# Two graph layers on one core: the second layer sums neighbours first and weights the sums per row tile

## What is computed

```
# layer 0 (T = 350 largest of each row are kept; no row of these inputs has more)
sim     = tanh(adj * adj)
new_adj = sim where adj > 0, at most T largest of a row
h2      = tanh(x @ W_proj + b_proj)
x1      = layernorm(x + relu(new_adj @ (h2 @ W_gcn) + b_gcn))
# layer 1
pos  = (adj > 0) @ x1
neg  = (adj < 0) @ x1
node = concat(pos, neg) @ node_weight + node_bias * diag(adj)
edge = (adj @ x1) @ edge_weight + edge_bias * diag(adj)
out  = layernorm(x1 + node + edge)
```

## Time and profile before

| | |
|---|---|
| runs | 654.3, 657.14, 657.41 us; median 657.14 |
| profiled execution | 656.15 us, span 653.9 us |
| TensorE, products / weight loads | 615.0 us (94%) / 348.3 us |
| VectorE | 492.2 us (75%) |
| ScalarE | 449.1 us (69%) |
| GpSimd | 122.3 us (19%), all in layer 0 |
| DMA | 130.62 MB, 200 GB/s over the span |
| mean granted TensorE clock | 0.981 |
| layer 0 products | 37.3 to 284.2 us |
| layer 1 | 284.2 us to the end |

### The profile page before, as it was taken

How to read it: one execution, slowest core, us unless ns; L and a number is a source line. 1 busy time by engine, 2 the same in 40 slices (tenths; PEclk the granted TensorE clock), 3 DMA queues, 4 the chain that set the end, 5 groups by cost and what they waited for, 6 DMA issues and landing times.

```text
span 653.9 us, 6778 instructions
## 1 busy us (share of the span) xinstructions
PE 615.0 (94%) x2016; PEld 348.3 (53%) x2016; DVE 492.2 (75%) x689; ACT 449.1 (69%) x302; POOL 122.3 (19%) x71
## 2 busy tenths in 40 slices
PE   6599599999999999999999999999999999999994
PEld 3454244444444444476655555555555555556993
DVE  2462797979797797995758978779688687786845
ACT  2295769797878879641688878787675858676740
POOL 0242446454454535400000000000000000000000
PEclk9699799999999999999999999999999999999997
DMA  9999999999999994000099888788675867765000
GB/s 210 335 209 245 243 331 321 267 305 258 295 257 311 259 286 130 1 1 0 25 254 238 256 248 232 240 220 249 189 212 161 240 198 203 203 181 145 1 17 18
DMA packets 140313, 130.62 MB, mean 200 GB/s; under 512 B 8579, under 2 KB 140294, under 8 KB 140294
## 3 DMA queue, kind: packets, MB, share of 16 engines
q1 hardware_dynamic: 72118, 65.23, 38.1%
q10 hardware_dynamic: 68176, 65.15, 36.0%
HBM read 128.27 MB, written 2.10 MB: 199 GB/s over the span
## 4 chain that ended last, share of the span: by engine, by line
PE 61%; issue 16%; POOL 13%; DVE 5%; ACT 2%; ACTq 2%; DMA 1%; POOLq 0%; SPq 0%; DVEq 0%
PE acc L950 29%; POOL a_cols L305 13%; PE acc L952 8%; PE acc L951 8%; DVE a_cols L495 3%; PE acc L892 3%; PE stage L914 2%; PE stage L970 2%; PE acc L970 2%; ACTq L380 2%; PE stage L843 1%; PE stage L836 1%; DMA early<-in_x_dram 1%; ACT a_cols L424 1%; DVE root L550 1%
## 5 line engine op out<-in xcount | busy, mean ns | idle before, releaser
L495 DVE STREAM_TRANSPOSE a_cols<-a_rows 128x2048 f32<-128x2048 f32 x128 | 293.1, 2302 | 88.8 <-PE acc L952 43.3
L892 PE MATMUL acc<-a_cols,rhs 128*128 128x512 f32 x512 | 224.9, 597 | 7.3 <-ACT a_cols L424 7.3
L950 PE MATMUL acc<-a_cols,rhs 128*128 128x512 f32 x448 | 229.0, 592 | 0.0
L951 PE MATMUL acc<-masks,pos_hi 128*128 128x512 f32 x224 | 178.5, 797 | 0.0
L448 ACT ACTIVATE a_rows<-a_rows 128x4096 f32<-128x4096 f32 x32 | 116.0, 3624 | 74.8 <-DVE a_cols L495 58.4
L892 PEld LDWEIGHTS acc<-a_cols,rhs 128*128 128x128 f32 x512 | 96.7, 192 | 123.9 <-issue 115.7
L305 POOL TENSOR_TENSOR a_cols<-a_cols 128x1024 f32<-128x1024 f32 x64 | 121.5, 1898 | 154.4 <-DVE a_cols L495 154.4
L424 ACT ACTIVATE a_cols<-a_cols 128x2048 f32<-128x2048 f32 x64 | 122.3, 1911 | 17.4 <-POOL a_cols L305 15.8
L451 ACT ACTIVATE a_rows<-a_rows 128x4096 f32<-128x4096 f32 x32 | 116.0, 3624 | 2.9
L950 PEld LDWEIGHTS acc<-a_cols,rhs 128*128 128x128 f32 x448 | 83.9, 189 | 19.3
L420 ACT ACTIVATE a_cols<-a_cols 128x1024 f32<-128x1024 f32 x64 | 67.1, 1049 | 35.4 <-DVE a_cols L495 18.5
(11 more groups left out here) (83 smaller groups left out, 326.4 us busy)
## 6 DMA issues: line engine op xcount, KB each, us to landing
a_rows<-in_adj_dram SPq DMA_DIRECT2D x120, 512.0 KB, 8.2
a_rows<-in_adj_dram ACTq DMA_DIRECT2D x120, 512.0 KB, 8.5
early<-in_x_dram SPq DMA_DIRECT2D x8, 256.0 KB, 6.3
out_dram<-n_rows ACTq DMA_DIRECT2D x7, 256.0 KB, 8.5
out_dram<-n_rows ACTq DMA_DIRECT2D x2, 128.0 KB, 1.8
w_pne<-n_L_gnn_node_weight_dram SPq DMA_DIRECT2D x1, 128.0 KB
w_pg<-in_L_gnn_W_proj_dram ACTq DMA_DIRECT2D x1, 64.0 KB, 2.7
w_pg<-in_L_gnn_W_gcn_dram ACTq DMA_DIRECT2D x1, 64.0 KB, 3.3
```

The source lines that it names most:

```text
L495: nc.vector.transpose(half_out(hs), half_in(s, h % HALVES)).then_inc(turned[layer], 1)
L892: last = nc.tensor.matmul(acc[parity][:], rhs[:, b, :], a_cols[:, h % HSLOTS, k, :], start=(b == 0), stop=(b == BLOCKS - 1))
L950: nc.tensor.matmul(acc[parity][:], rhs[:, b, :], cols, start=(b == 0), stop=False)
L951: nc.tensor.matmul(acc[parity][:], pos_hi[:, b, :], mask, start=False, stop=False)
```

## The change

The second layer is computed in another order: (A x1) W_edge + ((A > 0) x1) W_node, where it was A (x1 W_edge) + (A > 0)(x1 W_node). So `operands` is gone, x1 itself is the stationary operand, and each chunk's two sums (now in two banks, `acc` and `acc_m`) are copied to SBUF and multiplied with the weights tile by tile (`weigh`). A chunk is no longer 512 neighbouring rows but, for each of 16 sets, 32 rows out of 256, so that its rows are, in the order in which the columns lie on partitions, four whole blocks (c, c + 8, c + 16, c + 24). x lies in `x_rows` in that order, with rows on partitions; the layer norm writes x1 there, and nothing is transposed back. ScalarE rounds it into `x1_hi`, VectorE forms `x1_lo`, once per chunk in layer 0.

Also: GpSimd squares 1280 of 2048 elements of a half, where it was 1024, and ScalarE 768; x comes in 16 DMAs of 128 KB, half on SP and half on ScalarE's queue; ScalarE issues chunk 0's first piece before its first activation; the head goes through six banks in another order; the diagonal comes in four DMAs; the stores go out on SP, in four DMAs each.

```
-    SQ_POOL = HB // 2
+    SQ_POOL = HB * CH * 5 // 8
...
+        adj_sets = adj.rearrange("(r c i) k -> (c i) r k", c=CHUNKS, i=SQ)
+        x_blocks = x.rearrange("(q b j) f -> q j b f", q=QUARTERS, j=SQ)
+        def quarter_in(c, s, q):
+            return adj_sets[bass.ds(c * SQ, SQ), :, q * QUARTER + s * PCOLS:q * QUARTER + (s + 1) * PCOLS]
...
# ScalarE
+            def relu_out(chunk):
+                c, q, parity = chunk
+                act.wait_ge(half_used[0], HPC * (c + 1))
+                nc.scalar.activation(by_tile(z_t[:]), by_set(acc[parity][:]), ACT.Relu, bias=b_col[:, 1:2])\
+                    .then_inc(z_ready, 1)
+            def high_part(chunk):
+                c = chunk[0]
+                act.wait_ge(normed, c + 1)
+                nc.scalar.copy(rows_at(x1_hi, c), rows_at(x_rows, c)).then_inc(hi_ready, 1)
...
+                    nc.scalar.activation(rest, rest, ACT.Square).then_inc(squared_act, 1)
+                    if h == HPC - 1 and before:
+                        high_part(before)
...
-                if before:
-                    x1_back(before)
...
+                    if s == 1 and before:
+                        keep_sums(before)
+                    if s == 0 and not before:
+                        high_part(LAST)
# VectorE
+            def residual0(chunk):
+                c = chunk[0]
+                dve.wait_ge(rows_ready, c + 1)
+                nc.vector.tensor_tensor(y_rows[:], to_rows[:], rows_at(x_rows, c), ALU.add).then_inc(y_ready, 1)
+                dve.wait_ge(y_ready, c + 1)
+            def low_part(chunk):
+                c = chunk[0]
+                dve.wait_ge(hi_ready, c + 1)
+                nc.vector.tensor_tensor(rows_at(x1_lo, c), rows_at(x_rows, c), rows_at(x1_hi, c).bitcast(f32),
+                                        ALU.subtract).then_inc(lo_ready, 1)
...
                     turn(0, chunk[0], h)
-                    if h == 3 and before:
+                    if h == 4 and before:
                         residual0(before)
-                    if h >= 5 and before:
-                        norm0(before, h - 5)
+                        norm0(before, 0)
+                    if h == 5 and before:
+                        norm0(before, 1)
+                    if h == 6 and before:
+                        norm0(before, 2)
+                    if h == 7 and before:
+                        low_part(before)
...
+                nc.vector.tensor_copy(by_tile(sm_t[:]), by_set(acc_m[parity][:])).then_inc(sums_m_kept, 1)
# TensorE
                     last.then_inc(half_used[0], 1)
-                    if h == 1 and before:
-                        turn_to_rows(0, before[0])
-                    if h == 5 and before:
-                        turn_x1_back(before)
+                    if h == 0 and before:
+                        turn_to_rows(before)
...
+            def products(sums, sums_m, b, cols, mask):
+                nc.tensor.matmul(sums, x_rows[:, b, :], cols, start=(b == 0), stop=(b == BLOCKS - 1))
+                nc.tensor.matmul(sums_m, x1_hi[:, b, :], mask, start=(b == 0), stop=False)
+                return nc.tensor.matmul(sums_m, x1_lo[:, b, :], mask, start=False, stop=(b == BLOCKS - 1))
+            def weigh(rows, at, tiles):
+                for k in range(tiles):
+                    nc.tensor.matmul(rows[:, k, :], blk(z_t, at + k), w_pne[:, 2, :], start=True, stop=False)
+                    last = nc.tensor.matmul(rows[:, k, :], blk(sm_t, at + k), w_pne[:, 0, :], start=False, stop=True)
+                last.then_inc(rows_ready, 1)
+            def chunk_rows(chunk):
+                c = chunk[0]
+                pe.wait_ge(sums_kept, c + 1)
+                pe.wait_ge(sums_m_kept, c + 1)
+                pe.wait_ge(y_ready, CHUNKS + c)
+                weigh(to_rows, 0, TILES)
...
+                    if h == 0:
+                        chunk_rows(before)
```

More of the change, by code:

```diff
@@ L396, in _ @@
-            before_layer0(0)
-            def x1_back(chunk):
-                c, q, parity = chunk
-                act.wait_ge(cols_ready, c + 1)
-                nc.scalar.copy(nodes(feat_t[:], q, parity), sets(to_cols)).then_inc(x1_ready, 1)
+            act.wait_ge(proj_loaded, 32)
+            for n, (kind, g) in enumerate(USES):
+                if by_dve[n]:
+                    continue
+                act.wait_ge(staged, n + 1)
+                if kind == "hid":
+                    nc.scalar.activation(group(h_t, g), bank_of(n), ACT.Tanh, bias=b_col[:, 0:1])\
+                        .then_inc(stage_act, 1)
+                    if g in (1, 3, 6):
+                        load_piece(0, 1 + (1, 3, 6).index(g))
+                else:
+                    nc.scalar.copy(rhs[:, g * TILES:(g + 1) * TILES, :],
+                                   bank_of(n).rearrange("p (b f) -> p b f", f=F)).then_inc(stage_act, 1)
@@ L672, in layer1 @@
                         before_layer1(h)
+                    if h == 3 and before:
+                        keep_sums_m(before)
                     n, hs = turn(1, chunk[0], h)
@@ L676, in layer1 @@
                         .then_inc(masked, 1)
-                    if h == 3 and before:
-                        residual1(before)
                     if h >= 5 and before:
@@ L856, in turn_to_rows @@
+            def turn_to_rows(chunk):
+                c = chunk[0]
+                pe.wait_ge(z_ready, c + 1)
+                if not is_first(c):
+                    pe.wait_ge(y_ready, c)
                 for k in range(TILES):
@@ L858, in turn_to_rows @@
                 last.then_inc(rows_ready, 1)
-            def turn_x1_back(chunk):
-                c, q, parity = chunk
-                pe.wait_ge(normed, c + 1)
-                if not isinstance(c, int) or c > 0:
-                    pe.wait_ge(x1_ready, c)
-                for k in range(TILES):
-                    last = nc.tensor.transpose(to_cols[:, k * P:(k + 1) * P], n_rows[:, parity, k, :], ident[:])
-                last.then_inc(cols_ready, 1)
             def layer0(chunk, before):
@@ new lines, in chunk_rows, with first_chunk @@
+            def chunk_rows(chunk):
+                c = chunk[0]
+                pe.wait_ge(sums_kept, c + 1)
+                pe.wait_ge(sums_m_kept, c + 1)
+                pe.wait_ge(y_ready, CHUNKS + c)
+                weigh(to_rows, 0, TILES)
+            def first_chunk():
+                parity, late = 0, CHUNKS - 1
+                pe.wait_ge(lo_ready, late)
+                pe.wait_ge(masked, 1)
+                block_products(parity, 0, 0)
+                turn_to_rows(LAST)
+                for k in range(1, HB):
+                    last = block_products(parity, 0, k)
+                last.then_inc(half_used[1], 1)
+                pe.wait_ge(masked, 2)
+                for k in range(HB - 1):
+                    block_products(parity, 1, k)
+                pe.wait_ge(masked, 3)
+                for k in range(HB - 1):
+                    block_products(parity, 2, k)
+                pe.wait_ge(lo_ready, late + 1)
+                block_products(parity, 1, HB - 1).then_inc(half_used[1], 1)
+                block_products(parity, 2, HB - 1).then_inc(half_used[1], 1)
+                for h in range(3, HPC):
+                    pe.wait_ge(masked, h + 1)
+                    for k in range(HB):
+                        last = block_products(parity, h, k)
+                    last.then_inc(half_used[1], 1)
@@ L1005, in last_chunk @@
-                for h in range(apart + 1, HPC):
-                    last = products(h, 1)
-                last.then_inc(last_summed, 1)
-                turned_rows(1)
-            def sum_signs():
                 pe.wait_ge(stats_step, 1)
                 for q in range(QUARTERS):
-                    last = nc.tensor.matmul(stage[0][0:SQ, 0:CHUNKS], ident[:, q * SQ:(q + 1) * SQ], chunk_signs[:],
+                    last = nc.tensor.matmul(stats_at[0:SQ, 0:CHUNKS], ident[:, q * SQ:(q + 1) * SQ], chunk_signs[:],
@@ L1015, in sum_signs @@
                                             start=(q == 0), stop=(q == QUARTERS - 1))
                 last.then_inc(stats_pe, 1)
+                half_products(apart, 1)
+                pe.wait_ge(stats_step, 4)
+                nc.tensor.matmul(stats_at[0:1, CHUNKS:CHUNKS + 2], ones[:, 0:1], fails[:], start=True, stop=True)\
+                    .then_inc(stats_pe, 1)
+                part_rows(0)
+                for h in range(apart + 1, HPC):
+                    last = half_products(h, 1)
```

512 lines of the change are left out of this document (226 added, 286 removed).

## The result

| | before | after |
|---|---|---|
| median of the runs | 657.17 us (4) | 774.0 us (4; 767.68 to 784.0) |
| profiled execution / span | 656.15 / 653.9 us | 767.68 / 765.4 us |
| mean granted TensorE clock | 0.981 | 0.931 |
| chunk 1's first product | 72.3 us | 92.9 us |
| first product of layer 1 | 284.2 us (the operands) | 374.7 us |

The ratio is 1.176, 95% interval 1.164 to 1.187: 17.6% slower; it leaves out the run of 784.0 us, which lies 2.1% above the fastest, and the other three have the median 769.5 us. 673 us (645 to 685) was forecast: the side was right, the size and the cause of most of it were wrong. Of the profiled 111.5 us, the head has 20.6, the seven chunks after it 281.8 - 211.9 = 69.9, and layer 1 21.0.

A forecast was written before the change was run, and what follows sets the result against it. The prediction took TensorE to set the pace in layer 0, with one wait, and never to wait in layer 1. It summed 656.15 + 14 (layer 0) + 2.3 (layer 1) = 672.5, forecast 673 us, range 645 to 685.

The forecast's parts named there:

- rival 4: Layer 0's loads: rows 4 MB apart load slower, so DMA bounds a chunk; about 685 us, chance 0.04.
- Layer 0, +14: Six chunks of layer 0 at 32.4 us against 30.07, 2.35 us a chunk slower: +14 us.
- the scaling: VectorE's scaling of normalized rows in layer 0, now reading and writing SBUF: 1.06 us, excluding GpSimd meanwhile.
- the upper bound, 33.9 a chunk: Layer 0: GpSimd gets the ports between the first and second of four scaling instructions; 33.9 us a chunk, +22 us.
- (a): Layer 0: TensorE waits for ScalarE's relu before turning z to rows, 2.5 us by the walk; said to bind.
- (b): Layer 0, after half 7: VectorE waits for ScalarE's high part before the low part, 3.48 us; said to bind.
- Head, 0 (-4 to 4): Start until chunk 1: TensorE starts some 5 us earlier, then waits longer at chunk 1; priced at 0.
- Two queues: Head: x and the first piece go out on both queues; 0 by the skill, 2 to 3 us earlier by the row.
- Layer 1, +2.3: Layer 1: -14.8 for operand products and transposes, +9.4 weighting, +5.3 waits, +2.4 end: +2.3 us.
- The wait for the kept sums: Layer 1, chunk 1: TensorE waits for sums ScalarE keeps late, +4 us, not returning in later chunks.
- the one for the low part: Layer 1: TensorE reaches the late blocks before the last chunk's low part is there, +1.3 us.
- The sum: Whole kernel: 656.15 + 14 + 2.3 = 672.5, forecast as 673 us, 2.4% slower.

The follow-up runs named there:

- a_near: The changed kernel with its loads of adj taking 512 neighbouring rows as before (sets 32 rows apart): 687.04 us, one run.
- a_s64: The changed kernel with nodes renumbered so row sets lie 64 rows apart, diagonal transfers behind layer 0's loads, SP's quarters in order 1, 0: 671.85 us.

## Why the prediction was wrong, step by step

- **"The rows 4 MB apart load slower" (rival 4, chance 0.04, 685 us)** is the step that failed. It was the cause of 81 to 87 of the 117 us. Its price rested on "a chunk moves 8.4 MB in 30.07 us, 279 GB/s, against 347 seen; below 260 it binds": the need was right, and nothing in the trace of before bounded the rate of another address pattern, yet it was taken as nearly that seen. The measured rate was 194 to 203 in the middle of layer 0. The consequence was also cut short: slow issues stop ScalarE itself (88.5 us), which the sum had nowhere. The Trainium skill's row on pitches, quoted above, was there to make it a rival with a real chance; the prediction drew on another section of that page.
- **Layer 0, +14.** Without the far rows it was +25.5 us (a_near: 309.9 - 72.5 = 237.4 against 211.9). The mechanism was right, wait by wait: VectorE's for the high part 2.5 us (2.4 to 3.5 said), TensorE's for relu up to 2.2 (2.5 said), before half 0 1.84 (1.8 said), GpSimd's square 2.33 (2.37 said). The term mis-sized is the scaling, 3.08 us and not 1.06: "the steps in the trace that follow each other closely were not split" was the wrong reading, the upper bound, 33.9 a chunk, the right one. The middle chunks took 33.7 to 34.8 us.
- **(a) and (b) "both bind".** Half right: (b) cost 1.7 us a chunk, (a) nothing.
- **Head, 0 (-4 to 4).** With near rows right: chunk 1 begins at 72.5, 72.3 before; layer 0's first product comes at 28.2 in place of 37.3 (some 5 us earlier were said) and TensorE then waits 14.5 us for chunk 1, as forecast. What it named as hidden behind "the same 4096 single elements" was those elements themselves: 11 us to be had in the kernel before. With the far rows the head cost 20.6.
- **Two queues.** From 9 to 15 us a_near moves 302 GB/s, where the kernel before moved 217. But the prediction read the row as one queue against two, and the same trace does not bear that out. In the kernel before, SP's queue alone moved 314 GB/s from 7 to 10.2 us, and 192 GB/s from 10.5 to 15 us. By 10.2 us it had moved 2.1 MB, as much as x has, which goes to all 128 partitions; what followed were quarters 0 and 1, on partitions 0 to 63. So one queue is not what held the rate, and the row says nothing against the Trainium skill's rule ("DMA: Bandwidth & Descriptors", "Rules for kernel authors") that spreading over queues does not help. In a_near all four quarters move as well; no run parts the two. The faster start did not bring chunk 1 forward, because the diagonal held what follows.
- **Layer 1, +2.3.** +5.2 in a_near (374.9 against 369.7). The wait for the kept sums was there, in chunk 1 alone, 5.2 us where 4 was said, the one for the low part 1.2 where 1.3 was said; behind the wait the granted clock was 0.50 (1.2 GHz), so that in a_s64 the first weighting took 351.01 - 347.44 = 3.57 us and not 1.79. With the slow loads that wait grew to 17.7 us.
- **The sum.** 673 us is, by luck, almost the time of a_s64 (671.85): in its profiled execution the layers are 11 us dearer than forecast (+22.5 and +5.1 against +14 and +2.3) and the head 14 us cheaper.

## What to carry to other kernels

A change in which rows a transfer gathers is a change of its own, to be priced before any wait: measure the new pattern's rate first, above all if pieces lie a large power of two apart, and look for another numbering with the same algebra (here 64 rows in place of 256). In these runs a load that slowed down stopped the engine that issued it (88.5 us of "issue" on ScalarE), so large "issue" waits on an engine that issues loads are a reason to look at the DMA. Compare a new kernel also with the old one plus the side changes: here moving the diagonal alone gave 11 us. When a hold by GpSimd is removed at one step, look which of the next steps meets it.

## What the runs showed of the hardware that was not expected

- Transfers of 512 KB with pieces 32 and 64 rows of 16 KB apart land in 8.1 to 9.2 us (medians of a run), 128 apart in 13.6 to 15.1, 256 apart in 17.1 to 18.3, 240 apart in 8.3 to 8.8, and 255 apart in 11.8 to 13.5.
- A DMA issue on ScalarE took 10.71 us when loads were slow, and nothing behind it in ScalarE's program started before it was over.
- 4096 elements of 4 bytes beside large loads took these from 306 to 191 GB/s over 20 us.
- VectorE instructions that follow each other without a gap can be split by a GpSimd instruction: four that read SBUF took 3.08 us, where four that read PSUM took 1.32.
